# Four graphs at a time for q and k, one table turned over in place, single places for x and the product

## The chip, the cores and the metric

One NeuronCore of one Trainium2 chip runs the whole kernel. The metric is the device time of one execution in microseconds. Three executions of the kernel before took 2863.10, 2862.62 and 2861.37 us; the median is 2862.62.

## The reference

x is 128 graphs of 128 nodes with 512 features, adj is 128 matrices of 128x128. For each graph, in float32:

```python
q, k, v = split_heads(x @ Wq.T), split_heads(x @ Wk.T), split_heads(x @ Wv.T)   # 16 heads of 32
a = einsum('bhnd,bhmd->bhnm', q, k) * 512 ** -0.5 + 2 * adj
p = softmax(a)                                   # rows that are all zero give 0
x = layernorm(x + merge_heads(p @ v) @ Wo.T)
top1 = argmax(x.mean(1) @ router_w + router_b)   # one of 4 experts for a graph
out = adj @ (x @ expert_w[top1])
# batch norm over all nodes of all graphs of the same expert, then relu
x = layernorm(x + relu(batchnorm(out)))
```

## The kernel before, in words

The first part works through the graphs in *slots*, one for each graph, written by `run_slots` (L175): slots up to 7 straight out, slots 8 to 119 as a loop whose body is four slots, the rest straight out again. Each engine runs the same slots with its own list of work (`slot` at L225 for SP, L315 for POOL, L359 for PE, L509 for ACT, L609 for DVE), and semaphores hold them together. A slot t does different stages for different graphs: scores for graph t, transposes and attention times v for graph t-1, the output projection and the residual for graph t-2, adj times x and the router for t-3, the expert's product for t-4, v for graph t+2, and q and k for the next pair of graphs. After the last slot, a second part (`phase_two`, L720) works out the batch norm and finishes all graphs; the change leaves it alone.

Products in full precision are made of three float32r matmuls: each operand is split into a rounded part (`_hi`) and the rest (`_lo`), and `mm3` (L347) adds hi.hi, hi.lo and lo.hi over four blocks of 128 features, 12 matmuls in all.

In PE's slot the order is: scores (L364); two calls of `project_qk` (L378), each with q and k of one block c of features for the *pair* of graphs of the next slots, so 24 matmuls of 256 columns into one PSUM bank (q in its first half, k in its second); v (L439, 12 matmuls of 512 columns); 16 transposes of the softmax's result (L400); adj times x (L461); the output projection (L473, 12 of 512); the expert's product (L484 to L488, 12 of 512); the router (L497); attention times v (L414). In a pair of slots the two calls of each slot make the four blocks of the next pair. `qk` (L78) has two places of a pair each, and ACT copies a bank into it once for each block (`copy_qk`, L514).

x transposed comes in pairs of graphs (`load_xT`, L211) into one place, and POOL splits it into `xT_hi` and `xT_lo` (`split_xT`, L305), which have two places of a pair each. PE starts with slot -2: the pair of slots 0 and 1 is projected in slots -2 and -1. PE's first wait is for the third of the weights' splits on DVE (L587 to L591; L357); the weights wv, wq, wk, wo come in this order over SP's queue with the first pair of xT between wv and wq (L216 to L222).

The other tiles that the change touches: `x_in` (x for the residual, two places), `adj_in` and `adjT_in` (two places of two graphs, one DMA for two graphs), `conv` (the expert's product and its square, two places; ACT writes it at L576 and L577, POOL adds it to the moments at L326, SP stores it at L238).

Of the kernel before, what the change touches and what calls it, by code (L numbers as in the profile page):

```python
# [29 lines left out]
P = 128  # L30
# [4 lines left out]
def graph_block_program(nc, x, xT, adj, adjT, wqT, wkT, wvT, woT, router_w, router_b, expert_w,  # L35
# [7 lines left out]
    assert N == P and HD == 32 and B % 4 == 0 and B >= 20  # L43
# [6 lines left out]
    with ExitStack() as ctx:  # L50
# [38 lines left out]
        conv = sb("conv", [P, 2, 2, D])  # L89
# [23 lines left out]
        ld_x = [sem("ld_x0"), sem("ld_x1")]  # L113
# [3 lines left out]
        st_conv = [sem("st_conv0"), sem("st_conv1")]  # L117
# [55 lines left out]
        SLOT_LOOP_START, SLOT_LOOP_END, SLOT_END = 8, B - 8, B + 5  # L173

        def run_slots(eng, slot, first):  # L175


            for t in range(first, SLOT_LOOP_START):
                slot(t // 4, t % 4, lambda b: 0 <= b < B)
            with eng.Fori(SLOT_LOOP_START // 4, SLOT_LOOP_END // 4, 1) as i:  # L180
                for u in range(4):
                    slot(i, u, lambda b: True)
            for t in range(SLOT_LOOP_END, SLOT_END):
                slot(t // 4, t % 4, lambda b: 0 <= b < B)
# [10 lines left out]
        def quarter(i, u, k=0):  # L195

            return i + (u + k) // 4
# [12 lines left out]
        def _(sp):  # L210
# [14 lines left out]
            def slot(i, u, live):  # L225
# [9 lines left out]
                if live(b):  # L235
                    wait(sp, conv_copied, b + 1)
                    par = pv_mod(u, -5, 2)
                    sp.dma_start(conv_dram[:, bass.ds(b, 1), :].rearrange("p b d -> p (b d)"),  # L238
                                 conv[:, par, 0, :]).then_inc(st_conv[par], 16)
                if u % 2 == 0:  # L240
                    g = half(i, u)
                    pair = g + 1
                    if live(2 * pair):
                        par = (u // 2 + 1) % 2
                        wait(sp, biased, 8 * g)
                        sp.dma_start(adj_in[:, par, :, :], adj[bass.ds(2 * pair, 2), :, :].rearrange(
                            "b n m -> n b m")).then_inc(ld_adj[par], 16)
                    pair = g - 1
                    if live(2 * pair):
                        par = (u // 2 + 1) % 2  # L250
                        wait(sp, y_done, 2 * g - 4)
                        sp.dma_start(adjT_in[:, par, :, 0:P], adjT[:, bass.ds(2 * pair, 2), :]
                                     ).then_inc(ld_adjT[par], 16)
# [11 lines left out]
                if live(t):  # L265
                    wait(sp, residual_added, t - 1)
                    sp.dma_start(x_in[:, u % 2, :], x[bass.ds(t, 1), :, :].rearrange(
                        "b n d -> n (b d)")).then_inc(ld_x[u % 2], 16)
                if u % 2 == 0:
                    g = half(i, u)  # L270
                    if live(2 * (g + 3)) and (not isinstance(t, int) or g + 3 > 0):
                        load_xT(g + 3)
# [14 lines left out]
            for par in range(2):  # L287
                sp.wait_ge(st_x1[par], 16 * (B // 2))
                sp.wait_ge(st_conv[par], 16 * (B // 2))
# [3 lines left out]
        def _(pool):  # L293
            pool.memset(ident[:, :], 0.0).then_inc(pool_zeroed, 1)
            pool.memset(adjT_in[:, :, :, P:P + 1], 1.0 / N).then_inc(pool_ready, 1)
# [9 lines left out]
            def split_xT(pair, par):  # L305
                wait(pool, ld_xT, 16 * (pair + 1))
                wait(pool, v_done, 2 * pair - 2)
                wait(pool, qk_done, C * (pair - 1))
                pool.sem_inc(pool_passed)
                pool.tensor_copy(xT_hi[:, par, :, :], xT_in[:, :, :]).then_inc(x_rounded, 1)  # L310
                wait(pool, x_rounded, pair + 1)
                pool.tensor_tensor(xT_lo[:, par, :, :], xT_in[:, :, :],  # L312
                                   xT_hi[:, par, :, :].bitcast(F32), ALU.subtract).then_inc(x_split, 1)

            def slot(i, u, live):  # L315
# [3 lines left out]
                if live(b):  # L319
# [6 lines left out]
                    pool.tensor_tensor(acc, acc, conv[:, pv_mod(u, -5, 2), :, :].rearrange("p k d -> p (k d)"),  # L326
                                       ALU.add).then_inc(moments_added, 1)

                if u % 2 == 0:
                    pair = half(i, u) + 2  # L330
                    if live(2 * pair):
                        split_xT(pair, (u // 2) % 2)
# [10 lines left out]
        def _(pe):  # L343
# [15 lines left out]
            def slot(i, u, live):  # L359
                t = i * 4 + u  # L360
                pair = half(i, u)
                par = u // 2

                def scores():  # L364
                    if not live(t):
                        return
                    wait(pe, qk_copied, C * (pair + 1))
                    wait(pe, biased, HPC * t)
                    wait(pe, probT_copied, C * (t - 1))
                    side = u % 2 * P  # L370
                    for c in range(C):
                        for h in range(HPC):
                            rows = slice(HD * h, HD * h + HD)
                            last = mm(ps_heads[h][:, c * P:(c + 1) * P], qk[rows, par, c, 0, side:side + P],
                                      qk[rows, par, c, 1, side:side + P], True, True)
                    last.then_inc(scores_done, 1)

                def project_qk(c, dst):  # L378
                    nxt, npar = pair + 1, (par + 1) % 2
                    if not live(2 * nxt):  # L380
                        return
                    wait(pe, x_split, nxt + 1)
                    for i, k in enumerate("qk"):
                        last = mm3(dst[:, i * 2 * P:(i + 1) * 2 * P],
                                   [(w_hi[k][:, j, c * P:(c + 1) * P], w_lo[k][:, j, c * P:(c + 1) * P])
                                    for j in range(C)],
                                   [(xT_hi[:, npar, j, :], xT_lo[:, npar, j, :]) for j in range(C)])
                    last.then_inc(qk_done, 1)
# [33 lines left out]
                if live(2 * (pair + 1)):  # L422
# [4 lines left out]
                project_qk((2 * u) % C, ps_a)  # L427
                if live(2 * (pair + 1)):
                    if live(t - 3):
                        wait(pe, residual_added, t - 2)  # L430
                    else:
                        wait(pe, qk_copied, C * (pair + 1) + (2 * u) % C)
                project_qk((2 * u) % C + 1, ps_b)

                b = t + 2
                if live(b):
                    nxt, npar = pair + 1, (par + 1) % 2
                    wait(pe, qk_copied, C * nxt + (2 * u) % C + 1)
                    mm3(ps_a[:, :],  # L439
                        [(xT_hi[:, npar, j, u % 2 * P:u % 2 * P + P], xT_lo[:, npar, j, u % 2 * P:u % 2 * P + P])  # L440
# [8 lines left out]
                if live(b):  # L449
                    p4 = pv_mod(u, -3, 4)  # L450
                    wait(pe, x1_ready, b + 1)
                    wait(pe, ld_adjT[p4 // 2], 16 * (quarter(i, u, -3) + 1))
# [5 lines left out]
                    for c in range(C):  # L458
                        lhsT = x1[:, p4 % 2, c * P:(c + 1) * P]
                        dst = ps_c[:, c * Y:(c + 1) * Y] if c < C - 1 else ps_small[:, 0:Y]  # L460
                        last = mm(dst, lhsT, adjT_in[:, p4 // 2, p4 % 2, :], True, True)  # L461
# [3 lines left out]
                if live(b):  # L465
# [3 lines left out]
                    if live(2 * (pair + 1)):  # L469
                        wait(pe, qk_copied, C * (pair + 1) + (2 * u) % C + 2)  # L470
# [33 lines left out]
            run_slots(pe, slot, -2)  # L504
# [3 lines left out]
        def _(act):  # L508
            def slot(i, u, live):  # L509
                t = i * 4 + u  # L510
                pair, par = half(i, u), u // 2
                nxt, npar = pair + 1, (par + 1) % 2

                def copy_qk(c, src):  # L514
                    if live(2 * nxt):
                        wait(act, qk_done, C * nxt + c + 1)
                        wait(act, scores_done, 2 * (nxt - 1))
                        act.activation(qk[:, npar, c, :, :].rearrange("p k n -> p (k n)"), src[:, :],  # L518
# [27 lines left out]
                copy_qk((2 * u) % C, ps_a)  # L546
                copy_qk((2 * u) % C + 1, ps_b)
# [22 lines left out]
                if live(b):  # L570
                    p2 = u % 2
                    wait(act, conv_done, b + 1)
                    if not isinstance(t, int) or b // 2 > 0:
                        wait(act, st_conv[p2], 16 * half(i, u, -4))
                    wait(act, moments_added, b - 1)
                    act.activation(conv[:, p2, 0, :], ps_a[:, :], ACT.Copy).then_inc(conv_copied, 1)  # L576
                    act.activation(conv[:, p2, 1, :], ps_a[:, :], ACT.Square).then_inc(squared, 1)  # L577

            run_slots(act, slot, -2)
# [3 lines left out]
        def _(dve):  # L583
# [25 lines left out]
            def slot(i, u, live):  # L609
                t = i * 4 + u  # L610
                pair, par = half(i, u), u // 2
# [9 lines left out]
                if live(t):  # L621
                    wait(dve, scores_done, t + 1)
                    wait(dve, ld_adj[par], 16 * (quarter(i, u) + 1))
                    wait(dve, turned, C * (t - 1))
                    for h in range(HPC):
# [4 lines left out]
                            in1=adj_in[:, par, u % 2, :].unsqueeze(1).to_broadcast([P, C, P]),  # L630
# [42 lines left out]
                if live(b):  # L673
                    p2 = u % 2
                    wait(dve, proj_done, b + 1)
                    wait(dve, ld_x[p2], 16 * (half(i, u, -2) + 1))
# [360 lines left out]
```

## Time and profile before

| what | value |
|---|---|
| median of three runs | 2862.62 us |
| the profiled execution's own time | 2865.02 us |
| its span, first to last instruction | 2863.3 us |
| PE, weight loads, DVE, ACT, POOL busy | 94%, 83%, 74%, 63%, 27% |
| mean granted TensorE clock | 0.957 of 2.4 GHz |
| first part, from the first scores to the last slot | about 39 to 2535 us |
| second part | about 2535 to 2863 us |

The profile divides one execution by engine. A busy share says how long an engine had an instruction in flight; the start of one instruction to the start of the next says what each costs in a dense stream, since matmuls overlap. "Idle before, releaser" gives what an instruction waited for.

### The profile page before, as it was taken

The page shows a single profiled execution, that of the slowest core. Times are in us where ns is not written, and L with a number is a line of the kernel's source. Part 1 is how long each engine was busy: PE and PEld are TensorE (multiplying, and loading weights), DVE is VectorE, ACT ScalarE, POOL GpSimd, SP SyncE. Part 2 cuts the span into 40 slices and gives each one's busy share as a digit, 9 for nine tenths or more (in the row PEclk, how much of TensorE's full clock was granted, in tenths as well). Part 3 has the DMA queues.
Part 4 walks back from the last instruction along what each step waited for, and adds up shares of the span by engine and source line. Part 5 has one row for each costly group of instructions (what it writes and reads, how often), then busy time and mean ns, then how long its engine had stood idle before and what let it go on. Part 6 is the DMA issues. An engine that isn't in the chain of part 4 may idle for free. (4 is left out here: it accounts for less than half of the span.)

```text
span 2863.3 us, 70552 instructions
## 1 busy us (share of the span) xinstructions
PE 2685.5 (94%) x24130; PEld 2367.4 (83%) x24130; DVE 2114.0 (74%) x3938; ACT 1800.1 (63%) x6146; POOL 764.1 (27%) x431
## 2 busy tenths in 40 slices
PE   6999999999999999999999999999999999756765
PEld 6888888888888888888888888888888888545554
DVE  6877777777777777777777777777777777628776
ACT  3666666666666666666666666666666666528777
POOL 2133323322333232233323322333233222111110
PEclk9999999999999999999999999999999999867667
DMA  5445444444454454444444544454444444459887
GB/s 214 173 181 184 160 163 179 178 159 169 183 179 158 165 183 169 164 173 183 167 162 172 183 156 170 179 183 157 164 182 178 159 170 170 162 221 336 334 326 267
DMA packets 165114, 537.82 MB, mean 188 GB/s; under 512 B 15538, under 2 KB 48306, under 8 KB 122034
## 3 DMA queue, kind: packets, MB, share of 16 engines
q1 hardware_dynamic: 165042, 536.96, 51.2%
q8 instruction: 34, 0.56, 0.1%
q14 instruction: 38, 0.31, 0.0%
HBM read 427.84 MB, written 109.05 MB: 188 GB/s over the span
## 5 line engine op out<-in xcount | busy, mean ns | idle before, releaser
L532 ACT ACTIVATE prob<-prob,neg_max 128x128 f32<-128x128 f32 x2048 | 791.9, 394 | 5.3 <-DVE abs_max L654 5.3
L336 POOL TENSOR_TENSOR norm<-norm,constants 128x1 f32<-128x1 f32 x128 | 70.6, 551 | 1462.7 <-DVE norm L688 1462.7
L532 ACT ACTIVATION_READ_ACCUMULATOR prob<-prob,neg_max 128x1 f32 x2048 | 395.2, 193 | 0.0
L326 POOL TENSOR_TENSOR moments<-moments,conv 128x1024 f32 x128 | 310.7, 2427 | 293.7 <-ACT conv L577 195.0
L518 ACT ACTIVATE qk<-bank 128x512 f32<-128x512 f32 x256 | 152.7, 597 | 369.0 <-PE bank L345 369.0
L345 PE MATMUL bank<-xT_hi,wq_hi 128*128 128x256 f32 x1024 | 303.0, 296 | 19.7 <-DVE wk_lo L590 19.0
L626 DVE SCALAR_TENSOR_TENSOR prob<-bank,adj_in 128x512 f32<-128x512 f32 x512 | 316.7, 681 | 3.6 <-PE bank L345 3.6
L643 DVE TENSOR_TENSOR prob<-prob,inv_sum 128x2048 f32<-128x2048 f32 x128 | 293.4, 2292 | 4.4
L649 DVE TENSOR_REDUCE neg_max<-prob 128x16 f32<-128x2048 f32 x128 | 291.7, 2279 | 0.0
L654 DVE TENSOR_REDUCE abs_max<-prob 128x16 f32<-128x2048 f32 x128 | 291.7, 2279 | 0.0
L345 PE MATMUL bank<-xT_hi,wq_lo 128*128 128x256 f32 x1024 | 290.8, 284 | 0.0
L345 PE MATMUL bank<-xT_hi,wk_hi 128*128 128x256 f32 x1024 | 290.3, 283 | 0.0
L345 PE MATMUL bank<-xT_lo,wk_hi 128*128 128x256 f32 x1024 | 290.2, 283 | 0.0
L345 PE MATMUL bank<-xT_lo,wq_hi 128*128 128x256 f32 x1024 | 290.2, 283 | 0.0
L345 PE MATMUL bank<-xT_hi,wk_lo 128*128 128x256 f32 x1024 | 290.2, 283 | 0.0
L312 POOL TENSOR_TENSOR xT_lo<-xT_in,xT_hi 128x1024 fp32r<-128x1024 f32 x64 | 280.7, 4386 | 5.1
L525 ACT ACTIVATE probT<-bank 128x512 f32<-128x512 f32 x512 | 264.9, 612 | 18.2 <-PE bank L400 18.0
L400 PE MATMUL bank<-ident,prob 128*128 128x128 f32 x2048 | 249.7, 276 | 21.5 <-DVE prob L643 21.5
L400 PEld LDWEIGHTS bank<-ident,prob 128*128 128x128 f32 x2048 | 236.2, 143 | 38.7 <-DVE prob L643 23.0
L551 ACT ACTIVATE v<-bank 128x512 f32<-128x512 f32 x128 | 76.5, 597 | 279.0 <-PE bank L345 279.0
L576 ACT ACTIVATE conv<-bank 128x512 f32<-128x512 f32 x128 | 76.7, 599 | 259.9 <-PE bank L345 259.9
L345 PEld LDWEIGHTS bank<-xT_hi,wq_hi 128*128 128x128 f32 x1024 | 196.4, 192 | 35.5 <-issue 19.0
(111 smaller groups left out, 6516.3 us busy)
## 6 DMA issues: line engine op xcount, KB each, us to landing
expert_hi<-expert_hi_scratch SPq DMA_DIRECT2D x128, 1024.0 KB, 5.0
expert_lo<-expert_lo_scratch SPq DMA_DIRECT2D x128, 1024.0 KB, 7.0
xT_in<-xT SPq DMA_DIRECT2D x64, 512.0 KB, 3.5
x_in<-x SPq DMA_DIRECT2D x128, 256.0 KB, 2.6
x_scratch<-x SPq DMA_DIRECT2D x128, 256.0 KB, 2.1
conv_scratch<-conv SPq DMA_DIRECT2D x128, 256.0 KB, 2.3
conv_in<-conv_scratch SPq DMA_DIRECT2D x32, 1024.0 KB, 7.2
x_in<-x_scratch SPq DMA_DIRECT2D x32, 1024.0 KB, 9.2
```

Source lines behind the costliest of these rows:

```text
L312: pool.tensor_tensor(xT_lo[:, par, :, :], xT_in[:, :, :], xT_hi[:, par, :, :].bitcast(F32), ALU.subtract).then_inc(x_split, 1)
L326: pool.tensor_tensor(acc, acc, conv[:, pv_mod(u, -5, 2), :, :].rearrange("p k d -> p (k d)"), ALU.add).then_inc(moments_added, 1)
L345: return pe.matmul(dst, lhsT, rhs, start=start, stop=stop)
L400: last = pe.transpose(ps_heads[c][:, h * P:(h + 1) * P], prob[:, pv_mod(u, -1, 2), HPC * c + h, :], ident[:, :])
L518: act.activation(qk[:, npar, c, :, :].rearrange("p k n -> p (k n)"), src[:, :], ACT.Copy).then_inc(qk_copied, 1)
L525: act.activation(probT[:, HPC * c:HPC * (c + 1), :].rearrange("p h n -> p (h n)"), ps_heads[c][:, :], ACT.Copy).then_inc(probT_copied, 1)
L532: last = act.activation(prob[:, par2, h, :], prob[:, par2, h, :], ACT.Exp, bias=neg_max2[:, par2, h:h + 1], scale=2.0, accum_out=row_sum[: ...
L576: act.activation(conv[:, p2, 0, :], ps_a[:, :], ACT.Copy).then_inc(conv_copied, 1)
L626: dve.scalar_tensor_tensor(out=prob[:, u % 2, h:HEADS:HPC, :], in0=ps_heads[h][:, :].rearrange("p (c m) -> p c m", c=C), scalar=HALF_SCALE ...
L643: dve.tensor_tensor(prob[:, p2, :, :], prob[:, p2, :, :], inv_sum[:, :].unsqueeze(2).to_broadcast([P, HEADS, P]), ALU.mult).then_inc(norma ...
L649: dve.tensor_reduce(neg_max2[:, u % 2, :], prob[:, u % 2, :, :], AX.X, ALU.max, negate=True).then_inc(max_found, 1)
L654: dve.tensor_reduce(abs_max[:, u % 2, :], prob[:, u % 2, :, :], AX.X, ALU.max, apply_absolute_value=True).then_inc(abs_found, 1)
```

## The change

q and k are projected for four graphs at a time (a *quad*): `project` makes one block c of q, or of k, for four graphs with 12 matmuls of 512 columns into a bank of its own. Slot u of a quad makes q and k of block u for the next quad. The table `qk` holds one quad and is written over in place: with `side` 0 its first index is the graph and its second the block, with `side` 1 the other way round, so that the block that slot u writes goes where graph u was, whose scores this slot has just made. The loop's body becomes eight slots, and its end moves from B-8 to B-16. PE and ACT start at slot -4. `xT_hi` and `xT_lo` hold two quads; POOL splits the pairs in slots u = 2 and u = 3 instead of 0 and 2, and the first two pairs ahead of the slots, the second of them staged in `conv`, with a DMA of its own ahead of wq. `x_in` and `conv` have one place, `adj_in` and `adjT_in` two places of one graph, with one DMA for each graph.

```diff
-        xT_hi = sb("xT_hi", [P, 2, C, 2 * P], F32R)
-        xT_lo = sb("xT_lo", [P, 2, C, 2 * P], F32R)
-        x_in = sb("x_in", [P, 2, D])
-        adj_in = sb("adj_in", [P, 2, 2, P])
-        adjT_in = sb("adjT_in", [P, 2, 2, P + 1])
-        qk = sb("qk", [P, 2, C, 2, 2 * P])
+        xT_hi = sb("xT_hi", [P, 2, C, 4 * P], F32R)
+        xT_lo = sb("xT_lo", [P, 2, C, 4 * P], F32R)
+        x_in = sb("x_in", [P, D])
+        adj_in = sb("adj_in", [P, 2, P])
+        adjT_in = sb("adjT_in", [P, 2, P + 1])
+        qk = sb("qk", [P, 4, C, 2, P])
-        conv = sb("conv", [P, 2, 2, D])
+        conv = sb("conv", [P, 2, D])
...
-        SLOT_LOOP_START, SLOT_LOOP_END, SLOT_END = 8, B - 8, B + 5
+        SLOT_LOOP_START, SLOT_LOOP_END, SLOT_END = 8, B - 16, B + 5
...
+            with eng.Fori(SLOT_LOOP_START // 8, SLOT_LOOP_END // 8, 1) as i:
+                for side in range(2):
+                    for u in range(4):
+                        slot(i * 2 + side, u, side, lambda b: True)
...
+        def units(side, c, k):
+            return qk[:, :, c, k, :] if side == 0 else qk[:, c, :, k, :]
+        def graph_units(side, g, rows, c, k):
+            return qk[rows, g, c, k, :] if side == 0 else qk[rows, c, g, k, :]
...
                 if i == 1:
                     load_xT(0)
+                    sp.dma_start(conv[:, :, :].rearrange("p k d -> p (k d)"), xT[:, 1, :]).then_inc(ld_xT1, 16)
...
-                if live(t):
-                    wait(sp, residual_added, t - 1)
-                    sp.dma_start(x_in[:, u % 2, :], x[bass.ds(t, 1), :, :].rearrange(
+                b = t - 1
+                if live(b):
+                    wait(sp, residual_added, b)
+                    sp.dma_start(x_in[:, :], x[bass.ds(b, 1), :, :].rearrange(
...
+                if u >= 2:
+                    pair = i * 2 + u + 3
+                    if live(2 * pair):
+                        load_xT(pair)
...
+            split_xT(0, 0, 0, xT_in[:, :, :])
+            split_xT(1, 0, 1, conv[:, :, :].rearrange("p k (c n) -> p (k c) n", c=C // 2))
...
-                if u % 2 == 0:
-                    pair = half(i, u) + 2
-                    if live(2 * pair):
-                        split_xT(pair, (u // 2) % 2)
+                if u >= 2:
+                    pair = i * 2 + u + 2
+                    if live(2 * pair) and (not isinstance(t, int) or pair >= 2):
+                        split_xT(pair, side, u - 2, xT_in[:, :, :])
...
-                def project_qk(c, dst):
-                    nxt, npar = pair + 1, (par + 1) % 2
-                    if not live(2 * nxt):
+                def project(k, c, dst):
+                    if not quad_live:
                         return
-                    wait(pe, x_split, nxt + 1)
-                    for i, k in enumerate("qk"):
-                        last = mm3(dst[:, i * 2 * P:(i + 1) * 2 * P], ...
-                    last.then_inc(qk_done, 1)
+                    wait(pe, x_split, 2 * (i + 2))
+                    nxt = (side + 1) % 2
+                    mm3(dst[:, :],
+                        [(w_hi[k][:, j, c * P:(c + 1) * P], w_lo[k][:, j, c * P:(c + 1) * P]) for j in range(C)],
+                        [(xT_hi[:, nxt, j, :], xT_lo[:, nxt, j, :]) for j in range(C)]).then_inc(qk_done, 1)
...
-                project_qk((2 * u) % C, ps_a)
+                project("q", u, ps_a)
...
-                project_qk((2 * u) % C + 1, ps_b)
+                project("k", u, ps_b)
...
-                    wait(act, moments_added, b - 1)
-                    act.activation(conv[:, p2, 0, :], ps_a[:, :], ACT.Copy).then_inc(conv_copied, 1)
+                    wait(act, st_conv, 16 * b)
+                    wait(act, moments_added, b)
+                    act.activation(conv[:, 0, :], ps_a[:, :], ACT.Copy).then_inc(conv_copied, 1)
```

## Rows read from the trace of the kernel before

**Rows 1.** The page: busy time of each engine, its share, instructions.
```profile
PE 2685.5 (94%) x24130; PEld 2367.4 (83%) x24130; DVE 2114.0 (74%) x3938; ACT 1800.1 (63%) x6146; POOL 764.1 (27%) x431
```
**Rows 2.** Stretches between starts of scores: PE, PEld, DVE, ACT, POOL, clock, DMA share, GB/s.
```profile
39.25:123.77 84.52, 77.32 (x733) 67.68 (x733) 75.42 (x90) 49.12 (x185) 11.97 (x9) 0.96 0.55 202
123.77:2421.57 2297.80, 2297.80 (x21605) 2039.01 (x21601) 1728.18 (x3121) 1468.78 (x5281) 683.79 (x358) 1.00 0.47 171
2421.57:2440.72 19.15, 19.15 (x184) 16.98 (x181) 14.37 (x27) 12.24 (x45) 2.98 (x2) 1.00 0.40 152
2440.72:2458.49 17.77, 12.23 (x124) 10.55 (x120) 14.34 (x27) 10.88 (x42) 2.90 (x2) 0.81 0.47 171
```
**Rows 3.** PE's timeline in one steady slot: start us, duration us, engine, line, operation.
```profile
1215.23 1.17 PE L345 MATMUL bank<-qk 32*128 32x128 f32 x32
1216.33 0.39 PE L345 MATMUL bank<-xT_hi,wq_hi 128*128 128x256 f32 x1
1216.56 0.28 PE L345 MATMUL bank<-xT_lo,wq_hi 128*128 128x256 f32 x1
...
1222.07 0.28 PE L345 MATMUL bank<-xT_hi,wk_lo 128*128 128x256 f32 x1
1222.19 0.40 PE L345 MATMUL bank<-wv_hi,xT_hi 128*128 128x512 f32 x1
...
1223.35 0.39 PE L345 MATMUL bank<-wv_hi,xT_lo 128*128 128x512 f32 x1
...
1224.94 1.91 PE L400 MATMUL bank<-ident,prob 128*128 128x128 f32 x16
...
1227.50 0.48 PE L345 MATMUL bank<-wo_hi,oT_hi 128*128 128x512 f32 x1
1227.82 0.39 PE L345 MATMUL bank<-wo_lo,oT_hi 128*128 128x512 f32 x1
...
1230.38 0.39 PE L345 MATMUL bank<-expert_hi,yT_hi 128*128 128x512 f32 x1
...
1232.21 1.07 PE L345 MATMUL bank<-expert_lo,yT_hi 128*128 128x512 f32 x4
```
**Rows 4.** Waits of SP's queue, 400 to 2400 us: total us, times, longest.
```profile
SPq L267 <- DVE x L680: 1376.1, 105, 13.5
```
**Rows 5.** POOL's timeline in the same slot.
```profile
1216.14 2.43 POOL L326 TENSOR_TENSOR moments<-moments,conv 128x1024 f32 x1 [2.13 <-ACT conv L577]
1218.50 1.05 POOL L310 CAST xT_hi<-xT_in 128x1024 fp32r<-128x1024 f32 x1
1219.63 4.53 POOL L312 TENSOR_TENSOR xT_lo<-xT_in,xT_hi 128x1024 fp32r<-128x1024 f32 x1
```
**Rows 6.** Timeline of the start, idle time before and its releaser in brackets.
```profile
5.61 1.23 DVE L588 CAST wv_hi<-prob 128x2048 fp32r<-128x2048 f32 x1 [5.48 <-DMA prob<-wvT]
...
9.35 1.79 DVE L588 CAST wq_hi<-prob 128x2048 fp32r<-128x2048 f32 x1 [0.18 <-DMA prob<-wqT]
10.14 3.19 POOL L312 TENSOR_TENSOR xT_lo<-xT_in,xT_hi 128x1024 fp32r<-128x1024 f32 x1
11.17 4.31 DVE L590 TENSOR_TENSOR wq_lo<-prob,wq_hi 128x2048 fp32r<-128x2048 f32 x1
15.40 1.21 DVE L588 CAST wk_hi<-prob 128x2048 fp32r<-128x2048 f32 x1
...
16.65 2.29 DVE L590 TENSOR_TENSOR wk_lo<-prob,wk_hi 128x2048 fp32r<-128x2048 f32 x1
...
19.05 0.55 PE L345 MATMUL bank<-xT_hi,wq_hi 128*128 128x256 f32 x1 [19.05 <-DVE wk_lo L590]
...
24.88 2.40 POOL L312 TENSOR_TENSOR xT_lo<-xT_in,xT_hi 128x1024 fp32r<-128x1024 f32 x1
```
**Rows 7.** PE's timeline: an early slot's wait, and the wait of slot 126.
```profile
72.67 0.80 PE L345 MATMUL bank<-wv_hi,xT_hi 128*128 128x512 f32 x1 [3.08 <-ACT qk L518]
...
2447.43 3.53 PE L400 MATMUL bank<-ident,prob 128*128 128x128 f32 x16 [5.54 <-DVE prob L643]
```

More of the change, by code:

```diff
@@ L171, in graph_block_program @@
         expert_known = sem("expert_known")
-        SLOT_LOOP_START, SLOT_LOOP_END, SLOT_END = 8, B - 8, B + 5
+        SLOT_LOOP_START, SLOT_LOOP_END, SLOT_END = 8, B - 16, B + 5
         def run_slots(eng, slot, first):
             for t in range(first, SLOT_LOOP_START):
[L179 to L182, printed above, removed]
+                slot(t // 4, t % 4, t // 4 % 2, lambda b: 0 <= b < B)
+            with eng.Fori(SLOT_LOOP_START // 8, SLOT_LOOP_END // 8, 1) as i:
+                for side in range(2):
+                    for u in range(4):
+                        slot(i * 2 + side, u, side, lambda b: True)
             for t in range(SLOT_LOOP_END, SLOT_END):
-                slot(t // 4, t % 4, lambda b: 0 <= b < B)
+                slot(t // 4, t % 4, t // 4 % 2, lambda b: 0 <= b < B)
         def wait(eng, s, value):
@@ L224, in _, with slot @@
                 sp.dma_start(dst, src).then_inc(ld_const, 16)
-            def slot(i, u, live):
+            def slot(i, u, side, live):
                 t = i * 4 + u
@@ L288, in _ @@
                 sp.wait_ge(st_x1[par], 16 * (B // 2))
[L289 removed]
+            sp.wait_ge(st_conv, 16 * B)
         @block.gpsimd
@@ L303, in _, with split_xT, slot @@
             pool.wait_ge(pool_ready, READY - 1)
[L305 to L308, printed above, removed]
+            def split_xT(pair, par, at, staged):
+                if isinstance(pair, int) and pair == 1:
+                    pool.wait_ge(ld_xT1, 16)
+                else:
+                    wait(pool, ld_xT, 16 * (pair if not isinstance(pair, int) or pair else 1))
+                if at == 0:
+                    wait(pool, v_done, 2 * pair - 4)
+                    wait(pool, qk_done, 4 * pair - 8)
                 pool.sem_inc(pool_passed)
-                pool.tensor_copy(xT_hi[:, par, :, :], xT_in[:, :, :]).then_inc(x_rounded, 1)
+                part = slice(2 * P * at, 2 * P * at + 2 * P)
+                pool.tensor_copy(xT_hi[:, par, :, part], staged).then_inc(x_rounded, 1)
                 wait(pool, x_rounded, pair + 1)
-                pool.tensor_tensor(xT_lo[:, par, :, :], xT_in[:, :, :],
-                                   xT_hi[:, par, :, :].bitcast(F32), ALU.subtract).then_inc(x_split, 1)
-            def slot(i, u, live):
+                pool.tensor_tensor(xT_lo[:, par, :, part], staged,
+                                   xT_hi[:, par, :, part].bitcast(F32), ALU.subtract).then_inc(x_split, 1)
+            split_xT(0, 0, 0, xT_in[:, :, :])
+            split_xT(1, 0, 1, conv[:, :, :].rearrange("p k (c n) -> p (k c) n", c=C // 2))
+            def slot(i, u, side, live):
                 t = i * 4 + u
@@ L357, in _, with slot @@
             pe.wait_ge(w_split, 3)
-            def slot(i, u, live):
+            def slot(i, u, side, live):
                 t = i * 4 + u
-                pair = half(i, u)
-                par = u // 2
+                quad_live = live(4 * (i + 1)) if isinstance(t, int) else True
                 def scores():
@@ L366, in scores @@
                         return
-                    wait(pe, qk_copied, C * (pair + 1))
+                    wait(pe, qk_copied, 2 * C * (i + 1))
                     wait(pe, biased, HPC * t)
                     wait(pe, probT_copied, C * (t - 1))
-                    side = u % 2 * P
                     for c in range(C):
@@ L420, in slot @@
                 scores()
-                if live(2 * (pair + 1)):
+                copied = 2 * C * (i + 1) + 2 * u
+                if quad_live:
                     if live(t - 5):
@@ L426, in slot @@
                         wait(pe, v_copied, t + 2)
-                project_qk((2 * u) % C, ps_a)
-                if live(2 * (pair + 1)):
+                        wait(pe, qk_copied, copied - 1)
+                project("q", u, ps_a)
+                if quad_live:
                     if live(t - 3):
@@ L431, in slot @@
                     else:
-                        wait(pe, qk_copied, C * (pair + 1) + (2 * u) % C)
-                project_qk((2 * u) % C + 1, ps_b)
+                        wait(pe, qk_copied, copied)
+                project("k", u, ps_b)
                 b = t + 2
                 if live(b):
-                    nxt, npar = pair + 1, (par + 1) % 2
-                    wait(pe, qk_copied, C * nxt + (2 * u) % C + 1)
+                    xpar, at = (side + (u + 2) // 4) % 2, (u + 2) % 4 * P
+                    if quad_live:
+                        wait(pe, qk_copied, copied + 1)
+                    else:
+                        wait(pe, squared, t - 4)
                     mm3(ps_a[:, :],
-                        [(xT_hi[:, npar, j, u % 2 * P:u % 2 * P + P], xT_lo[:, npar, j, u % 2 * P:u % 2 * P + P])
+                        [(xT_hi[:, xpar, j, at:at + P], xT_lo[:, xpar, j, at:at + P])
                          for j in range(C)],
@@ L468, in slot @@
                         pe.wait_ge(w_split, 4)
-                    if live(2 * (pair + 1)):
-                        wait(pe, qk_copied, C * (pair + 1) + (2 * u) % C + 2)
+                    if quad_live:
+                        wait(pe, qk_copied, copied + 2)
                     else:
@@ L502, in slot, with copy_projected @@
                     times_v(c)
-            run_slots(pe, slot, -2)
+            run_slots(pe, slot, -4)
         @block.scalar
         def _(act):
-            def slot(i, u, live):
+            def slot(i, u, side, live):
                 t = i * 4 + u
[L511 to L518, printed above, removed]
+                quad_live = live(4 * (i + 1)) if isinstance(t, int) else True
+                def copy_projected(k, c, src):
+                    if quad_live:
+                        wait(act, qk_done, 2 * C * (i + 1) + 2 * c + k + 1)
+                        wait(act, scores_done, t + 1)
+                        act.activation(units((side + 1) % 2, c, k), src[:, :].rearrange("p (g n) -> p g n", g=4),
                                        ACT.Copy).then_inc(qk_copied, 1)
@@ L570, in slot @@
                 if live(b):
-                    p2 = u % 2
                     wait(act, conv_done, b + 1)
-                    if not isinstance(t, int) or b // 2 > 0:
-                        wait(act, st_conv[p2], 16 * half(i, u, -4))
-                    wait(act, moments_added, b - 1)
-                    act.activation(conv[:, p2, 0, :], ps_a[:, :], ACT.Copy).then_inc(conv_copied, 1)
-                    act.activation(conv[:, p2, 1, :], ps_a[:, :], ACT.Square).then_inc(squared, 1)
-            run_slots(act, slot, -2)
+                    if isinstance(t, int) and b == 0:
+                        act.wait_ge(x_split, 2)
+                    wait(act, st_conv, 16 * b)
+                    wait(act, moments_added, b)
+                    act.activation(conv[:, 0, :], ps_a[:, :], ACT.Copy).then_inc(conv_copied, 1)
+                    act.activation(conv[:, 1, :], ps_a[:, :], ACT.Square).then_inc(squared, 1)
+            run_slots(act, slot, -4)
         @block.vector
@@ L607, in split_expert, with slot @@
                     dve.memset(moments[:, :], 0.0).then_inc(moments_cleared, 1)
-            def slot(i, u, live):
+            def slot(i, u, side, live):
                 t = i * 4 + u
-                pair, par = half(i, u), u // 2
                 b = t - 2
@@ L675, in slot @@
                     wait(dve, proj_done, b + 1)
-                    wait(dve, ld_x[p2], 16 * (half(i, u, -2) + 1))
+                    wait(dve, ld_x, 16 * (b + 1))
                     wait(dve, y_done, b - 1)
```

72 lines of the change are left out of this document (31 added, 41 removed).

## The prediction

> **What bounds the kernel now.** I read the page's busy shares first, then windows cut at the starts of the scores, then PE's timeline in one slot, then SP's waits and POOL's timeline, and the two ends last. PE is the busiest engine [rows 1]; the windows say why. From slot 5 (123.77 us) to slot 125 (2421.57) are 120 slots in 2297.80 us, 19.15 each; PE is busy in all of that time, with a granted clock of 1.00, while DVE has 1728 us of work and ACT 1469 [rows 2]. So in these slots a nanosecond less on PE is a nanosecond less of time, until another engine ends last. The two ends are otherwise. In slots 0 to 4 (84.52 us) DVE is busy for 75.42 and PE waits. In slot 126, which has no projection left, the slot takes 17.77 us with PE busy for 12.23: PE waits 5.54 us for DVE's normalised rows, and the clock falls [rows 2, 7].
>
> **The steady slot.** q and k of a slot run from 1216.33 to 1222.19 [rows 3]: 48 matmuls in 5.86 us. The first step, behind the scores, is 0.23 us; the other 47 take 5.63, or 119.8 ns each for 256 columns. Columns alone are 106.7 ns at the granted 2.4 GHz, so each matmul carries some 13 ns beside its columns. Half as many matmuls of twice the width halve that part. What a 512-column matmul costs is shown by three groups [rows 3]:
> - v: 12 in 2.75 us (1222.19 to 1224.94), 229.2 each. The first five steps take 1.16 us (232), the last seven 1.59 (227).
> - the expert's product: 8 in 1.83 us (1230.38 to 1232.21), 228.8.
> - the output projection: 11 in 2.56 us (1227.82 to 1230.38), 232.7.
>
> Two of three settle near 227, which is 213.3 of columns and the same 13 to 14 ns. The new q and k are one stream of 24 with the same kinds of operands as v's, and v follows in the same stream. I take v's pattern: 5 x 0.232 + 19 x 0.227 = 5.47, and 0.11 for the first step behind the scores as now, 5.58; v then runs settled, 12 x 0.227 = 2.72 in place of 2.75. Gain per slot: 0.28 + 0.02 = 0.30 us. Ends: 24 x 232.7 + 0.11 = 5.69, a gain of 0.17 (the output projection's pace); and 226.7 all through, 0.34.
>
> The Trainium skill (TensorE: Matmul & The Clock Gate, section "Wait — 56ns, not 53.3ns?") puts the fixed cost of a warm matmul at about 2.5 ns. By that, a slot would gain 24 x 2.5 = 60 ns. The trace disagrees at both widths (13 to 14 ns, [rows 3]), and it decides; what the rule would make of the time is a rival below.
>
> **What else the steady slot gets.** The rest of PE's list is the same. Slots 5 to 123 keep their projections: 119 x 0.30 = 35.7 us.
> - ACT still copies two banks a slot, now with strided output of runs of 128; I cost it at nothing, as ACT has 36% of the stretch idle [rows 2].
> - Turning the table over adds a wait on the scores of the same slot. It is on ACT, behind q's matmuls, which run after these scores on PE; nothing waits.
> - One place for x: its DMA is issued at the same point of SP's list, behind the residual of graph t-2. SP already waits up to 13.5 us there [rows 4]; the load has then a whole slot before DVE wants it.
> - One place for the product: ACT writes it at the end of a slot; POOL has read the one before from 1216.14 to 1218.57, 15 us earlier [rows 5].
> - POOL's splits in two adjacent slots: each starts behind the moments and ends at 1224.16, 10 us before the next slot (1234.38 = 1215.23 + 19.15) [rows 5, 2]. The later one, in slot u = 3, is the one PE's next slot waits for. That cover would fail at 10 us more.
> - Two more small DMAs each two slots cost SP about 0.4 us each, out of its 13 us of waiting [rows 4].
>
> **The start.** PE's first matmul waits for wk_lo on DVE and starts at 19.05 [rows 6]. Now 0.5 MB of xT stand ahead of wq, and POOL splits a second pair. wv (1 MB) had landed at 5.61 and the next 1.5 MB at 9.35: 0.5 MB is 1.25 us, so wq lands at 10.6. The second term is that DVE and POOL hold each other up. wq_lo took 4.31 us from 11.17, against 2.29 for the same shape in wk_lo; the 2.02 more are POOL's xT_lo, which ran to 13.33 [rows 6]. Taking turns: POOL's xT_lo for pair 0 (10.14, 2.40 alone) ends at 12.5, and from there DVE has 1.21 + 2.29 + 1.21 + 2.29 = 7.0 us and POOL 1.05 + 2.40 = 3.45 for pair 1 [rows 5, 6], all in a row 10.5: 23.0, or 4.0 us later. Ends: 1.3 (the DMA alone) and 4.5.
>
> The Trainium skill (SBUF — State Buffer, section "Who interferes with whom") calls the pair of ports of the two engines an exclusive lock. The trace agrees, by the 2.02 us; a sharing of bandwidth would give less than 4.0.
>
> Then PE projects a whole quad before slot 0: 96 matmuls of 512 columns where there were 96 of 256. 96 x 0.228 - 96 x 0.120 = 10.4 us more; v of two graphs is in both. ACT's copies hide behind the next bank's matmuls (2.7 us against one copy). Slots 0 to 4 I leave at 84.5 us, since DVE sets them [rows 2] and its list there is unchanged; PE's gain is not booked.
>
> **The end.** q and k for all graphs are now done four slots before the last, so slots 124 and 125 lose 5.86 us of PE's work each, but the chain from scores to normalised rows stays. Slot 126 had 17.77 with a cold clock behind the 5.54 us wait: 16 transposes there took 3.53 us against 1.91 [rows 7, 3], so 16.2 with a warm one. In slots 124 and 125 v fills 2.75 of the 5.54 us; the wait left, 2.8, is near the 3.08 of [rows 7] behind which v's first step is in the slow clock (0.80 us against 0.40). I take 17.0: 2 x (19.15 - 17.0) = 4.3 us gained; ends 2.8 and 5.9.
>
> **Sum.** +4.0 + 10.4 - 4.3 - 35.7 = -25.6 us. The profiled execution's own time is 2865.0 (span 2863.3), 2.4 above the median of 2862.6; against the median the forecast is 2837.0.
>
> **Rivals.**
> 1. *q and k run at the output projection's pace*, 232.7 ns, without settling. For it: that group never settles, with operands of the same shape. Against: v and the expert do. Gain 0.17 x 119 = 20.2, the prologue 96 x 0.1127 = 10.8: -9.7, so 2853.
> 2. *Small fixed cost*: 60 ns a slot. 7.1 us gained in 119 slots, prologue 96 x 0.1175 = 11.3: +3.9, 2866, no change that can be measured. It is the skill's rule above; the rows speak against it.
> 3. *Slower, by columns*: a 512-column matmul of this stream costs what two of 256 do, 240 ns. Then nothing is gained and the front stays: +4.0 + 11.5 - 4.3 = +11.2, 2874. It decides from a gain under 0.09 us a slot, a pace above 236 ns. No group in [rows 3] is that slow after its first steps, though new addresses could be.
> 4. *Slower, by the loop's edge*: the body is eight slots, 13 turns in place of 28. The edge costs nothing now: 120 slots with PE at 100% [rows 2]. If the longer code made PE wait at each turn, break-even is at 2.0 us a turn; at a wait like the early one of 3.08 [rows 7] it is 13 x 3.08 = 40 us, 2877.
>
> **How the numbers follow.** Forecast 66%, its own range 2829 to 2846 (gain 0.25 to 0.34, start and end at their bounds); rival 1 16%; rival 2 6%; rival 3 5%; rival 4 4%; the rest, 3%, is a start or early slots that cost more than I booked. A change of 0.2% is 5.7 us, so faster is below 2856.9 and slower above 2868.3. Faster 0.82 (forecast and rival 1), same 0.09 (rival 2 and the rest), slower 0.09. Range 2828 to 2858: the low end is the forecast's with all terms good, the high end takes in rival 1 with a start at 4.5 and an end at 2.8.
>
> **What would show it.** In the profile after: starts of q and k 227 to 229 ns apart, slots of 18.85 us, PE at 100% with clock 1.00 from slot 5 to slot 123; PE's first matmul near 23 us; scores of graph 0 near 53 (39.25 + 4.0 + 10.4); slots 124 and 125 near 17. It would be wrong if steps of 232 or more last through the groups, if a wait on x_split, conv or x_in stands in PE's or DVE's rows, if slots at the loop's edge are longer than the rest, or if slots 0 to 4 grow beyond 85 us.

## The result and the profile after

The changed kernel takes 2947.61 us (median of 4 runs) against 2862.41 for the kernel before: a ratio of 1.0295, 95% interval 1.0282 to 1.0307. The forecast was 2837.0. The profiled execution has a span of 2947.7 us, against 2863.3. The page's busy times answer to [rows 1]:

```profile
PE 2683.1 (91%) x21058; PEld 2232.6 (76%) x21058; DVE 2113.6 (72%) x3938; ACT 1801.6 (61%) x6146; POOL 764.5 (26%) x431
```

PE has 3072 matmuls fewer and nearly the same busy time; DVE, ACT and POOL have the same work. The span grew, so something new is waited for.

**The steady slot is as forecast.** The same view as [rows 3], PE's timeline in slot 9 of the changed kernel:

```profile
212.71 1.17 PE L360 MATMUL bank<-qk 32*128 32x128 f32 x32
213.81 0.50 PE L360 MATMUL bank<-xT_hi,wq_hi 128*128 128x512 f32 x1
214.15 0.39 PE L360 MATMUL bank<-xT_lo,wq_hi 128*128 128x512 f32 x1
...
216.67 0.39 PE L360 MATMUL bank<-xT_hi,wk_hi 128*128 128x512 f32 x1
...
219.39 0.39 PE L360 MATMUL bank<-wv_hi,xT_hi 128*128 128x512 f32 x1
```

q takes 2.86 us with its first step of 0.34, k 2.72 us, or 226.7 ns a matmul. q and k together are 5.58 us (213.81 to 219.39) against 5.86.

**Some slots are long.** Windows cut at the starts of scores (columns as in [rows 2]): eleven slots ahead of the first jump back of the loop, the last slot of the loop's body, and the first one of the next turn:

```profile
118.52:325.73 207.21, 207.21 (x1721) 173.15 (x1717) 159.62 (x293) 134.67 (x484) 58.44 (x32) 1.00 0.49 175
325.73:348.61 22.88, 18.91 (x160) 15.74 (x157) 15.65 (x31) 13.85 (x51) 10.83 (x5) 1.00 0.54 197
348.61:372.08 23.47, 21.48 (x157) 17.73 (x158) 13.12 (x22) 10.64 (x39) 0.55 (x1) 0.85 0.30 103
```

Eleven slots in 207.21 us are 18.84 each, with PE at 100% and the clock at 1.00. Then come 22.88 and 23.47. From slot 5 to the start of slot 124 there are 95 slots of 18.83 to 18.85 and 24 long ones, two at each of the loop's 12 jumps back. The excess over 18.84 is 112.2 us in all, 9.3 a jump (7.8 to 10.3). (From here on, a *jump* is a jump back to the start of the loop's body, and the *excess* is the time of the long slots beyond that of a steady slot.) PE's timeline at the first jump:

```profile
343.60 1.04 PE L360 MATMUL bank<-probT,v 128*32 128x128 f32 x29
348.61 0.98 PE L360 MATMUL bank<-qk 32*128 32x128 f32 x13 [3.97 <-issue]
351.58 1.65 PE L360 MATMUL bank<-qk 32*128 32x128 f32 x19 [1.99 <-issue]
353.16 0.80 PE L360 MATMUL bank<-xT_hi,wq_hi 128*128 128x512 f32 x1
353.75 0.63 PE L360 MATMUL bank<-xT_lo,wq_hi 128*128 128x512 f32 x1
```

The releaser is "issue": PE waits for no semaphore that the profile shows. The second hole is in the middle of one group of scores, where the program has no wait at all. After the holes the matmuls are in the slow clock (0.80 and 0.63 us against 0.50 and 0.39 above), and the group of 12 q matmuls takes longer for it. The 24 holes of the loop add up to 71.7 us, so about 40 us of the 112.2 are not holes; in the second slot of the first jump the granted clock was 0.85.

The view of the DMA queues over the loop (400 to 2300 us; packets, MB, share of the 16 engines) has the other half. The kernel before has one queue there:

```profile
q1 hardware_dynamic: 105566, 324.43, 46.9%
```

and the changed kernel three:

```profile
q1 hardware_dynamic: 102686, 311.63, 45.0%
q8 instruction: 146, 2.39, 0.6%
q14 instruction: 71, 0.58, 0.1%
```

Over this stretch code is fetched all through the changed loop, and not at all in the loop before. q8's packets are 2.39 MB / 146 = 16 KB each, q14's 8 KB. The holes are therefore read as waits for PE's own instructions; that q8 is PE's queue is seen in `b_pe_body8` below, and which engines q14 serves isn't shown. Up to here that is an argument from two views; the experiments make it a finding.

**The ends** answer to [rows 6, 7]. The start:

```profile
10.67 2.94 DVE L602 CAST wq_hi<-prob 128x2048 fp32r<-128x2048 f32 x1 [1.46 <-DMA prob<-wqT]
...
14.59 4.26 POOL L324 TENSOR_TENSOR xT_lo<-conv,xT_hi 128x1024 fp32r<-128x1024 f32 x1
...
19.96 2.29 DVE L604 TENSOR_TENSOR wk_lo<-prob,wk_hi 128x2048 fp32r<-128x2048 f32 x1
...
22.36 0.76 PE L360 MATMUL bank<-xT_hi,wq_hi 128*128 128x512 f32 x1 [22.36 <-DVE wk_lo L604]
```

and slot 124, whose transposes wait for DVE's normalised rows:

```profile
2497.89 1.97 PE L410 MATMUL bank<-ident,prob 128*128 128x128 f32 x16 [2.59 <-DVE prob L656]
```

### The profile page after: what moved, and what is told of

It reads as the page before. It is cut to its first block and busy times, and to the rows that moved or that the text cites. A ratio compares the mean times of both kernels' runs of the same rounds, so it can differ in the third digit from the quotient of the medians.

```text
span 2947.7 us, 64325 instructions
## 1 busy us (share of the span) xinstructions
PE 2683.1 (91%) x21058; PEld 2232.6 (76%) x21058; DVE 2113.6 (72%) x3938; ACT 1801.6 (61%) x6146; POOL 764.5 (26%) x431
## 5 line engine op out<-in xcount | busy, mean ns | idle before, releaser
L360 PE MATMUL bank<-xT_hi,wq_hi 128*128 128x512 f32 x512 | 224.5, 438 | 23.0 <-DVE wk_lo L604 22.4
L360 PE MATMUL bank<-qk 32*128 32x128 f32 x4096 | 170.3, 298 | 71.7 <-issue 71.7
L360 PEld LDWEIGHTS bank<-qk 32*128 32x128 f32 x4096 | 141.3, 198 | 101.6 <-issue 101.6
L360 PE MATMUL bank<-expert_hi,yT_hi 128*128 128x512 f32 x512 | 202.2, 395 | 12.7 <-DMA expert_hi<-expert_hi_scratch 12.7
L693 DVE TENSOR_TENSOR x<-bank,x_in 128x512 f32<-128x512 f32 x128 | 88.5, 691 | 173.5 <-PE bank L360 173.5
L360 PE MATMUL bank<-wo_hi,oT_hi 128*128 128x512 f32 x512 | 212.5, 415 | 0.0
L360 PE MATMUL bank<-xT_lo,wq_hi 128*128 128x512 f32 x512 | 208.2, 407 | 0.0
```

The source lines that it names most:

```text
L360: return pe.matmul(dst, lhsT, rhs, start=start, stop=stop)
L693: dve.tensor_tensor(x1[:, p2, :], ps_b[:, :], x_in[:, :], ALU.add).then_inc(residual_added, 1)
```

## The experiments

Theory C: at each jump back PE waits for its own code, because a body of eight slots is longer than what PE keeps, while one of four is not. Rivals: S, the schedule at the turn of two quads (the side, a semaphore) makes the long slots; C-others, the code of another engine (ACT or DVE) is what is late, since a second queue, q14, also has packets in the loop. Where no number of runs is given below, there is one run.

**All engines straight out.** `a_straight`:

```diff
-            with eng.Fori(SLOT_LOOP_START // 8, SLOT_LOOP_END // 8, 1) as i:
-                for side in range(2):
-                    for u in range(4):
-                        slot(i * 2 + side, u, side, lambda b: True)
+            for t in range(SLOT_LOOP_START, SLOT_LOOP_END):
+                slot(t // 4, t % 4, t // 4 % 2, lambda b: 0 <= b < B)
```

> The changed kernel with no loop on any engine: slots 8 to 111 written straight out, the same instructions in the same order. Theory C (code): at each of the 12 jumps back of the changed kernel PE waits for its own instructions, since the eight-slot body is longer than what PE keeps; the 24 long slots add 112 us to 96 of 18.84. Without a jump back all slots are 18.84 and the time is 2947.6 - 112 = about 2836. Rival S (schedule): the long slots come from the change of side or from a wait at the turn of two quads; these are unchanged, so the time stays at 2947.

Measured: 2842.89 us (4 runs, 2835.83 to 2847.16), ratio to the kernel before 0.9928, interval 0.9910 to 0.9947. By the medians that is 22.0 us less than the kernel before on the same chip (2864.84). The profiled execution is the fastest, 2835.83. A window of its steady slots, and its queues from 400 to 2300 us:

```profile
135.32:2355.39 2220.07, 2220.07 (x18366) 1855.42 (x18363) 1702.94 (x3062) 1443.84 (x5191) 669.02 (x351) 1.00 0.49 175
```
```profile
q8 instruction: 127, 2.08, 0.5%
q14 instruction: 84, 0.69, 0.1%
```

No slot is long; PE is busy in all of the 2220.07 us. S falls: sides and semaphores are the same. Straight code is fetched as well, 127 packets of it, and PE never waits in this stretch: what costs is the jump, not the fetching.

**One engine at a time.** `a_pe_straight` and `a_others_straight` have the loop above in an `if eng is nc.tensor` and its opposite.

```diff
+            if eng is nc.tensor:          # "is not" in a_others_straight
+                for t in range(SLOT_LOOP_START, SLOT_LOOP_END):
+                    slot(t // 4, t % 4, t // 4 % 2, lambda b: 0 <= b < B)
+            else:
+                with eng.Fori(SLOT_LOOP_START // 8, SLOT_LOOP_END // 8, 1) as i: ...
```

> The changed kernel with slots 8 to 111 written straight out on PE alone; SP, POOL, ACT and DVE keep the eight-slot loop. Theory C-PE: PE's own code is what is late; 2836, perhaps up to 15 us more if another engine's jump also shows. Rival C-others: the code of ACT or DVE, whose instruction queue also has packets at the jumps, is what is late; then this stays near 2947.

> The changed kernel with the eight-slot loop on PE alone; the four other engines have slots 8 to 111 straight out. Theory C-PE: PE still waits about 9 us at each of 12 jumps; 2947, perhaps 5 us less. Rival C-others: 2836.

Measured: 2841.66 with PE alone straight, 2949.01 with PE alone in the loop. In the first the longest slot of the loop is 19.71 us and most of those at the other engines' jumps are 18.9 to 19.1. In the second the 24 long slots are there again, 108.8 us of excess, with the same two holes:

```profile
349.75 1.22 PE L364 MATMUL bank<-qk 32*128 32x128 f32 x13 [4.79 <-issue]
352.77 1.65 PE L364 MATMUL bank<-qk 32*128 32x128 f32 x19 [1.79 <-issue]
```

C-others falls: the other engines' jumps lengthen a slot by 0.9 us at most, PE's own by 3 to 7 us.

**The longer body alone, in the kernel before.** `b_pe_body8`:

```diff
+            if eng is nc.tensor:
+                with eng.Fori(SLOT_LOOP_START // 8, SLOT_LOOP_END // 8, 1) as i:
+                    for side in range(2):
+                        for u in range(4):
+                            slot(i * 2 + side, u, lambda b: True)
+            else: ...                     # the four-slot loop as it was
```

> The kernel before with nothing changed but PE's loop: a body of eight slots and 14 turns in place of four slots and 28 turns; the instructions that run are the same. Theory C-PE: the body is now longer than what PE keeps, 13 jumps back at about 9.3 us each are 121 us, so 2983. Rival S: nothing happens, 2862.

Measured: 2946.17 us, against 2864.84 for the kernel before on the same chip. The direction is as theory C has it, the size is less: 26 long slots at 13 jumps, 80.4 us of excess, 6.2 a jump in place of 9.3. There is one hole a jump here, and code comes in, on q8 alone. Only PE's loop was changed, so q8 is PE's:

```profile
340.05 2.09 PE L351 MATMUL bank<-qk 32*128 32x128 f32 x32 [3.69 <-issue]
```
```profile
q8 instruction: 160, 2.62, 0.6%
```

The instructions that run are those of the kernel before, in their order. The longer body of PE's loop by itself costs 81 us. Why the changed kernel has two holes at a jump and this one has one wasn't tried.

**Fewer jumps.** `a_body16`:

```diff
-        SLOT_LOOP_START, SLOT_LOOP_END, SLOT_END = 8, B - 16, B + 5
+        SLOT_LOOP_START, SLOT_LOOP_END, SLOT_END = 16, B - 16, B + 5
...
+            with eng.Fori(SLOT_LOOP_START // 16, SLOT_LOOP_END // 16, 1) as i:
+                for k in range(4):
+                    for u in range(4):
+                        slot(i * 4 + k, u, k % 2, lambda b: True)
```

> The changed kernel with a loop of sixteen slots from slot 16 to slot 111: 6 turns, 5 jumps back, in place of 12. If each jump costs a fixed 9.3 us whatever the body's length: 2836 + 47 = 2883. Rival: what is fetched anew at a jump grows with the body, so that a jump costs twice as much: 2836 + 93 = 2929.

Measured: 2878.64 us. 10 long slots at 5 jumps, 44.0 us of excess, 8.8 a jump: so the price goes with the number of jumps and is about the same for a body twice as long.

**How long a body may be.** The size of PE's code can be had from what straight code fetches. The kernel before straight out (`b_straight`, the same edit as `a_straight`) fetched 143 packets of 16 KB in 1900 us, 23.6 KB a slot, so its four-slot body is about 95 KB; the changed kernel's eight slots are about 165 KB. (A KB is 1000 bytes here, except that a packet of 16 KB is 16,384 bytes.) Four kernels lie between. `a_hi_all` leaves the lo products out, of the expert's product too (not shown):

```diff
-                    mm(dst, lh, rh, i == 0, False)
-                    mm(dst, lh, rl, False, False)
-                    last = mm(dst, ll, rh, False, i == n - 1)
+                    last = mm(dst, lh, rh, i == 0, i == n - 1)
...
```

> The changed kernel with its eight-slot loop, the lo products left out of q, k, v, the output projection and the expert's product (one matmul in place of three). PE's list falls from 160 to 120 matmul records a slot. Straight code fetched 127 blocks of 16 KB in 1900 us, 20.6 KB a slot; in proportion the body falls from 165 to 124 KB. The body that showed no jump cost is 4/8 of the 184-record one, about 95 KB. If PE keeps 128 KB, this body fits: no packets on PE's instruction queue in the loop, and no waits at the jumps. If it keeps less, 12 jumps with waits as before. Slots are set by DVE here, about 16 to 17 us.

Measured: 2696.76 us, and the body was not kept: packets go on through the loop, and PE waits for "issue" at each of the 12 jumps, 3.0 to 4.6 us. Slots are set by other chains here, so this run says whether code is fetched, not what that costs:

```profile
324.07 1.60 PE L360 MATMUL bank<-qk 32*128 32x128 f32 x32 [3.14 <-issue]
```
```profile
q8 instruction: 117, 1.92, 0.4%
```

The other three are the kernel before with scores made again, which lengthens a four-slot body and changes no result:

```diff
-                    for c in range(C):
+                    for c in (*range(C), *range(C // 2)):     # b_scores15
...
+                    for again in range(2):                    # b_scores2; range(3) in b_scores3
+                        for c in range(C): ...
```

> The kernel before with its four-slot loop; half of the scores' matmuls are made a second time, into the same places with the same values, to lengthen PE's list from 184 to 200 matmul records a slot. Straight code of the kernel before fetched 143 blocks of 16 KB in 1900 us, 23.6 KB a slot; in proportion the four-slot body grows from 95 to 103 KB. Measured so far: a body of 95 KB costs nothing at its jump, one of about 124 KB does. If the border is near 96 KB: 27 jumps with waits, about 8 us each, over 3050 us. If it is above 103 KB: no packets on PE's instruction queue in the loop, slots longer by 16 records (some 0.55 us): about 2930.

> As the kernel with half of the scores made twice, but all of them: 216 records a slot, a body of about 111 KB. If the border is at 112 KB or above: no packets in the loop, slots longer by 1.1 us, about 3000. If it is below: 27 jumps with waits besides, over 3150.

> As before with all scores made three times: 248 records a slot, a body of about 127 KB. If the border lies below 124 KB, as the run without the lo products has it, there are 27 jumps with waits: slots longer by 2.2 us and 27 times about 8 us, near 3360. Rival: that run's waits came from something else in it, and a body just under 128 KB is kept: no packets, about 3140.

Measured, each beside 2865.88 for the kernel before: 2917.97, 2992.53 and 3265.52 us. Slots without a hole are 19.60, 20.04 and 20.94. `b_scores3` came out below the 3360 expected: the slots grew by 1.8 us in place of 2.2, and a jump cost 6.7 in place of 8. The queues of `b_scores2` and of `b_scores3`, 400 to 2300 us (`b_scores15` has q1 alone there):

```profile
q1 hardware_dynamic: 100026, 308.06, 44.5%
q8 instruction: 18, 0.29, 0.1%
```
```profile
q1 hardware_dynamic: 89376, 275.29, 40.1%
q8 instruction: 210, 3.44, 0.8%
```

| kernel | body on PE, as expected ahead of the runs | the same by PE's instructions | jumps back | PE's packets, 400 to 2300 us | excess of long slots, us |
|---|---|---|---|---|---|
| before | 95 KB | 97 KB | 27 | 0 | 0 |
| b_scores15 | 103 KB | 105 KB | 27 | 0 | 0 |
| b_scores2 | 111 KB | 113 KB | 27 | 18 | 20.0, at 3 jumps |
| a_hi_all | 124 KB | 128 KB | 12 | 117 | not readable |
| b_scores3 | 127 KB | 130 KB | 27 | 210 | 180.4, at 27 jumps |
| changed | 165 KB | 169 KB | 12 | 146 | 112.2 |
| b_pe_body8 | 189 KB | 193 KB | 13 | 160 | 80.4 |

The first column of sizes goes by the packets of straight code, and for kernels that weren't run straight by proportion of matmuls. The second counts PE's instructions in the traces (matmuls, weight loads, and those of its sequencer): `b_straight` has 369 a slot for its 23.6 KB, or 64 bytes each; `a_straight` has 321 for 20.6 KB, the same. A loop needs a few more, because it works out in registers what it waits for: 378 a slot in the kernel before, 330 in the changed one, 506 in `b_scores3`. Both columns are estimates; the second is used from here on.

The border for PE is between some 113 and 128 KB. At 113 KB the loop waited at three early jumps and then fetched nothing from 600 us on; why it settled isn't shown. The price of a jump that missed was 6.2 to 9.3 us here (6.7 in `b_scores3`). The kernels with scores made again have the jumps and the register work of the kernel before, and only the body is longer, so a jump or the work at it is not what costs by itself.

The Trainium skill (Runtime: NRT & Kernel Launch, section "Instruction fetch mechanics") gives PE 128 KiB of instruction memory, filled in blocks of 16 KiB, and says that a taken branch to a target outside a window of two such blocks makes the engine wait for a fetch. The packets of 16 KB and the waits at jumps agree. The window of two blocks does not: bodies of 97 and 105 KB had no wait at their 27 jumps, and no packet from 400 to 2300 us. 128 KiB are 131 KB, and `b_scores3`'s body, 130 KB, is just under that and missed at every jump. Whether less than the 128 KiB is usable, or whether whole blocks are kept and this body lies across nine of them, no run shows.

**The change without its loop.** For `b_straight`:

> The kernel before with all engines' slots 8 to 119 straight out. Its four-slot loop showed no long slot, so going straight should give nothing: 2862, within 5 us. If instead straight code is itself faster (rival), this falls below 2855 and part of what the changed kernel's straight version gained over the kernel before is not the change's. In steady stretches its slots are 19.15, those of the changed kernel 18.84.

Measured: 2871.82 us (10 runs), ratio to the kernel before 1.0025, interval 1.0015 to 1.0034: straight code is no gain in itself, and slightly slower. Its slots are 19.15 as before. Its profiled execution is longer by 5.3 us behind the last scores (410.1 against 404.8), 1.5 in slots 0 to 4 and 1.1 in slot 126; why wasn't followed up. The change less its loop is worth about 0.9928 / 1.0025 = 0.990; the two ratios are from two chips.

**A version that beats both.** `a_best` is `a_straight` with PE's first wait split:

```diff
-            pe.wait_ge(w_split, 3)
+            pe.wait_ge(w_split, 2)
...
+                if t == -4:
+                    pe.wait_ge(w_split, 3)
                 project("k", u, ps_b)
```

> The changed kernel straight out on all engines, and PE's first wait split: PE begins q's block 0 behind wq's split, and waits for wk's split ahead of k's block 0. In the changed kernel PE began at 22.36 behind wk_lo, while the second pair of xT was split at 18.85. Theory: PE begins at about 18.9, the scores of graph 0 come 2.5 to 3.5 us earlier, and so does the end: about 2833. Rival: DVE sets slots 0 to 4 and its splits of wo and of the first expert are late then, so nothing is gained: 2836.

Measured: 2839.26 us (4 runs, 2834.54 to 2841.93), ratio 0.9911, interval 0.9890 to 0.9932. PE starts 3.4 us earlier and the scores of graph 0 come at 48.8 in place of 52.8:

```profile
19.00 0.77 PE L358 MATMUL bank<-xT_hi,wq_hi 128*128 128x512 f32 x1 [19.00 <-POOL xT_lo L322]
```

The profiled execution gives that back: slots 124 and 125 are 17.85 us in place of 16.19, and the stretch behind the last scores is 410.0 in place of 406.9. The intervals of `a_best` and `a_straight` overlap, so the split wait is not shown to help; both beat the kernel before by 0.7 to 0.9%.

## Why the prediction was wrong, point by point

**The step that failed** is the one that wasn't costed: the loop's body of eight slots. It stood as rival 4 with 4% and was dismissed with "the edge costs nothing now: 120 slots with PE at 100%". That row was about a four-slot body. It bounds nothing for one 1.75 times as long, and the trace held no jump to code that isn't kept, so no row had a price for one. The 3.08 us that rival 4 used is an early wait of PE for ACT, another kind of wait. Rival 4's mechanism was the true one; its price, 13 turns at 3.08 us or 40 us in all, was low as well. There are 12 jumps at 9.3 us, 112 in all: two holes of 4 and 2 us at the first one, and behind them matmuls in the slow clock.

A view would have raised the chance: the queues of the kernel before show no instruction packet from 400 to 2300 us in its loop, while its whole run has 34 of them on q8. So the loop ran from code that was kept, and how much can be kept was an open question, not a settled one.

**The sum, term by term**, against the profile of the kernel before:

| term | forecast, us | measured, us | from |
|---|---|---|---|
| PE's first matmul later | +4.0 | +3.3 | 22.36 - 19.05 |
| prologue longer | +10.4 | +10.9 | 31.06 - 20.20 |
| slots 0 to 4 | 0 | -0.6 | 83.95 - 84.52 |
| slots 5 to 123, the projections | -35.7 | -36.7 | 119 x (19.148 - 18.84) |
| slots 5 to 123, jumps back | 0 | +112 | 24 long slots |
| slots 124 and 125 | -4.3 | -5.9 | 32.38 - 38.28 |
| behind the last scores | 0 | +1.7 | 406.5 - 404.8 |

The rows add up to +84.7, and the spans differ by 84.4; slot 126 is 0.1 shorter, and the rest is rounding. Without the jumps' row they give -27.3, where the forecast had -25.6. `a_straight`'s profiled execution, 2835.8 us against 2865.0, is -29.2, but it is the fastest of four; the medians differ by 22.0. So the other terms are right to a few us, and the runs don't say more.

**What was right.** 512-column matmuls of q and k settle at 227 ns, and v behind them too. Rivals 1 to 3 are out with that: 232.7 was not the pace, 2.5 ns was not the fixed cost (13 ns beside the columns at either width), and 240 did not occur. The turns of DVE and POOL at the start came out as worked, 0.7 us shorter. None of the single places made PE wait: it is busy in every moment of `a_straight`'s steady stretch. Slots 124 and 125 were at the good end of their range, because the clock held: 16 transposes behind a wait of 2.59 us took 1.97 us, not 3.53. That is in part luck: `a_best` has the same wait there, its clock fell (0.90 over each of these slots), and both took 17.85. The forecast's 17.0 lies between the two outcomes.

## What to carry to other kernels

A longer loop body is a cost term of its own: before a body grows, look at the instruction queues in the view of DMA queues over the loop. No packets there means that the code is kept, and the size of the body can be estimated from what straight code of the same kernel fetches for each unit of work. On PE a body of about 105 KB was kept, one of 113 KB missed three early jumps, and those of 128 KB or more missed at every jump, at 6 to 9 us each where the price could be read. Straight code takes the cost away; fewer and longer turns cut it (44 us at 5 jumps in place of 112 at 12). A row in which something costs nothing bounds it only for its own size.

## What the runs showed of the hardware

- Waits for code appear as idle time with the releaser "issue", in the middle of a group of matmuls too (3.97 and 1.99 us at the changed kernel's first jump). When only PE's loop was lengthened, q8 alone had packets, of 16 KB.
- Straight code costs PE nothing in steady slots even at 100% busy: 1.26 packets of 16 KB in a slot of 18.84 us, with no idle time in 2220 us.
- The pace of a stream of equal matmuls can settle: in the changed kernel the steps of q's 512-column matmuls behind the first (336 ns) take 228 to 236 ns, then 227 for as long as the stream lasts (q's last five, all of k's and nearly all of v's). The output projection's, 232.7 in [rows 3], doesn't settle; why wasn't tried.
